# Another order of TensorE's work in the attention loop of a fused attention and mixture-of-experts kernel

## Chip, cores and metric

One core of a Trainium2 chip. The metric is the device time of one execution in microseconds (us). Engines: TensorE (PE, its weight loads PEld), VectorE (DVE), ScalarE (ACT), GpSimd (POOL) and SyncE (SP), which issues most of the transfers.

## What is computed

x is [8, 16, 16, 256]: eight images of 256 positions. First a layer norm over channels and axial attention (every position attends to its row and to its column, with a Gaussian decay), projected and added to x; then a layer norm and a top-1 switch gate over 8 experts with 256 places each.

```python
q, k, v = (xn @ W.T + b for W, b in ((Wq, bq), (Wk, bk), (Wv, bv)))
r_attn = softmax(einsum('bhwd,bhkd->bhwk', q, k) - gw * dist(w))
c_attn = softmax(einsum('bhwd,bgwd->bwhg', q, k) - gw * dist(h))
x = x + ((r_attn @ v) + (c_attn @ v)) @ Wo.T + bo
idx = argmax(softmax(t @ wg))                  # t = layer norm of x, one token a row
loc = cumsum(one_hot(idx), axis=0) - 1         # place of a token at its expert, below 256
out = x + gate * (relu(di @ w1[e]) @ w2[e])    # di: the tokens of expert e
```

## The kernel before

The kernel has a preparation (weights folded together), a loop over the eight images (the attention and the gate), and then the eight experts. The change is in the loop over images; each engine has its program written out by hand, and semaphores tie them together. Image i is two tiles of 128 positions.

TensorE's helpers for an image i (line numbers as in the trace):

- transpose_x(i) (L599): four transposes of the normalised image `xn` into the PSUM bank bank_xT. ScalarE copies them to xT_high (L859), VectorE subtracts to get xT_low (x_low, L1070).
- query(i) (L580, L581, L587 into bank_q): twelve matmuls in three passes for each half (high x high, high x low, low x high). The third pass of the first half waits for xT_low.
- scores(i) (the same lines into bank_s): twelve matmuls of query and transposed x. VectorE's maxima(i) (L1124, L1127) read them, ScalarE takes the exponentials (L883, L884), and VectorE's weights(i) (L1137 to L1140) joins row and column weights into e_col.
- transpose_prob(i) (L639): four transposes of e_col into bank_pT, copied by ScalarE (L870).
- values(i) (into banks_v): twelve matmuls of 274 columns, copied by ScalarE (L890). It waits for v_ready >= i and for count_read >= i - 1.
- attention_out(i, t), "the product" (L650 into banks_o): weights times values, eight matmul instructions in all. VectorE's residual(i, t) (L1154) reads it and makes the row of the new x.
- counts(i) (L661 to L665): five small matmuls that count, from the chosen experts of image i and of those before, how many tokens chose each expert. Their output is ps_count, a piece of the bank of the values, or, with late=True, ps_count_late, a piece of bank_xT. Without late it also waits for v_ready >= i + 2.

VectorE's turn i is: x_low(i + 1), maxima(i), place(i - 2), weights(i), query_low(i + 1), residual(i - 1), choose(i - 1). choose (L1162 to L1167) takes the maximum of the gate's logits (lmax), `ranked`, rmax and `chosen`. place (L1173 to L1181) forms `both`, multiplies the counts out of PSUM (`counted`, which raises count_read), and ends in `slot`.

ScalarE's turn i is: transposed_x(i + 1), normalised_x(i + 2), transposed_prob(i - 1), exponentials(i), query(i + 1), one piece of an expert weight, values(i).

GpSimd works for i = 2 to 7 on: pre_residual(i - 1) (four small operations, L461 to L465, behind ScalarE's copy of the values), x_and_bias(i) (L471, waits for xT_high_ready >= min(i + 2, 8) and for x2_ready >= 2 (i - 1), the residuals of image i - 2), for i = 3 to 6 a piece of expert 1's weights (L487), and scatter_rows(i - 2) (two indirect DMAs, L478, behind `slot`).

The loop of TensorE runs over i = 1 to 6 (B is 8); the last image is done after it. The expert phase behind it begins with the rows that the last images send.

Of the kernel before, what the change touches and what calls it, by code (L numbers as in the profile page):

```python
# [33 lines left out]
B, HH, WW, D = 8, 16, 16, 256  # L34
# [17 lines left out]
EARLY = B - 2  # L52
# [37 lines left out]
def wait(eng, sem, value):  # L90

    if isinstance(value, int) and value <= 0:
        return
    eng.wait_ge(sem, value)
# [18 lines left out]
def build(nc, x, Wq, bq, Wk, bk, Wv, bv, Wo, bo, sigma, wg, w1, w2, tables_in, eye, tokens, slots, out):  # L113
    f32, f32r, bf16, i32, u32 = mybir.dt.float32, mybir.dt.float32r, mybir.dt.bfloat16, mybir.dt.int32, mybir.dt.uint32
    ALU, ACT, AX = mybir.AluOpType, mybir.ActivationFunctionType, mybir.AxisListType

    ctx = ExitStack()
    with ctx:
        def sb(name, shape, dt=f32):
            return ctx.enter_context(nc.sbuf_tensor(name, shape, dt))  # L120
# [4 lines left out]
        def sem(name):  # L125
            return ctx.enter_context(nc.semaphore(name))
# [58 lines left out]
        chosen = sb("chosen", [P, 2, E], bf16)  # L185
        both = sb("both", [P, E], bf16)
        before = [sb(f"before{j}", [P, E], bf16) for j in range(2)]
        counted, loc = sb("counted", [P, 2, E]), sb("loc", [P, 2])
# [22 lines left out]
        def halves(a):  # L211
            return a.rearrange("p (a b) -> p a b", a=2)
# [6 lines left out]
        ps_count = halves(ps_v[:, 0, MW:MW + 2 * E])  # L219
        ps_count_late = halves(bank_xT[:, 0:2 * E])  # L220
# [47 lines left out]
        chosen_ready, count_made, count_read, slot_ready = (sem(n) for n in ("chosen_ready", "count_made", "count_read", "slot_ready"))  # L268
# [37 lines left out]
        def pT_of(i, t):  # L306
            return ps_pT_last[t] if i == B - 1 else ps_pT
# [256 lines left out]
        def _(pe):  # L564
# [6 lines left out]
            def three_passes(out_ap, stationary, moving, last="moving", before_last=None, before_pair=None):  # L571


                n = len(stationary)
                for c in range(n):
                    (a_h, a_l), (b_h, b_l) = stationary[c], moving[c]
                    second = (a_h, b_l) if last == "stationary" else (a_l, b_h)
                    if before_pair and c % 2 == 0:
                        before_pair(c // 2)
                    nc.tensor.matmul(out_ap, a_h, b_h, start=c == 0, stop=False)  # L580
                    nc.tensor.matmul(out_ap, *second, start=False, stop=False)  # L581
                if before_last:
                    before_last()
                for c in range(n):
                    (a_h, a_l), (b_h, b_l) = stationary[c], moving[c]
                    third = (a_l, b_h) if last == "stationary" else (a_h, b_l)
                    step = nc.tensor.matmul(out_ap, *third, start=False, stop=c == n - 1)  # L587
                return step
# [4 lines left out]
            def transpose_x(i):  # L593

                pe.wait_ge(xn_ready, i + 1)
                wait(pe, xT_ready, i)
                for t in range(2):
                    for c in range(DC):
                        step = nc.tensor.transpose(ps_xT[:, c, t * P:(t + 1) * P], xn[:, t, c * P:(c + 1) * P], ident)  # L599
                step.then_inc(xT_made, 1)  # L600

            def query(i):
                j = i % 2
                pe.wait_ge(xT_high_ready, i + 1)
                wait(pe, q_ready, i)
                for d in range(DC):
                    step = three_passes(ps_q[:, d, :], [(a_high[:, c, chunk[d]], a_low[:, c, chunk[d]]) for c in range(DC)],
                                        [(xT_high[j][:, c, :], xT_low[j][:, c, :]) for c in range(DC)],
                                        before_last=(lambda: pe.wait_ge(xT_ready, i + 1)) if d == 0 else None)
                step.then_inc(q_made, 1)  # L610

            def scores(i):

                j = i % 2
                pe.wait_ge(q_high_ready, i + 1)
                wait(pe, top_ready, 4 * i)
                for t in range(2):
                    three_passes(scores_of(i, t), [(qT_high[:, c, chunk[t]], qT_low[:, c, chunk[t]]) for c in range(DC)],
                                 [(xT_high[j][:, c, :], xT_low[j][:, c, :]) for c in range(DC)], last="stationary",
                                 before_last=(lambda: pe.wait_ge(q_ready, i + 1)) if t == 0 else None).then_inc(s_made, 1)  # L620

            def values(i, which=range(2)):

                j = i % 2
                wait(pe, v_ready, i)
                wait(pe, count_read, i - 1)
                for t in which:
                    step = three_passes(ps_v[:, t, 0:MW], [(xT_high[j][:, c, chunk[t]], xT_low[j][:, c, chunk[t]]) for c in range(DC)],
                                        [(m_high[:, c, :], m_low[:, c, :]) for c in range(DC)])
                    if t == 1 or i == B - 1:  # L630
                        step.then_inc(v_made, 1)

            def transpose_prob(i, which=range(2)):

                wait(pe, pT_ready, 2 * i)
                for t in which:
                    pe.wait_ge(u_ready, 2 * i + t + 1)
                    for c in range(2):
                        step = nc.tensor.transpose(pT_of(i, t)[:, c, t * P:(t + 1) * P], e_col[:, t, c * P:(c + 1) * P], ident)  # L639
                    step.then_inc(pT_made, 1)  # L640

            def attention_out(i, t):

                pe.wait_ge(pT_ready, 2 * i + (t + 1 if i == B - 1 else 2))
                pe.wait_ge(v_ready, i + 1 + (i == B - 1))
                wait(pe, x2_ready, 2 * (i - 1) + t + 1)
                if i == 0:
                    pe.wait_ge(b_ready, 1)
                for c in range(2):
                    step = nc.tensor.matmul(ps_o[:, t, 0:VW], pT[:, c, t * P:(t + 1) * P], v_sb[i % 2][:, c, 0:VW], start=c == 0, stop=c == 1)  # L650
                step.then_inc(o_made, 1)

            def counts(i, late=False):

                pe.wait_ge(chosen_ready, i + 1)
                wait(pe, before_ready, i)
                wait(pe, count_read, i)
                if not late:
                    pe.wait_ge(v_ready, i + 2)
                ps, b = ps_count_late if late else ps_count, before[i % 2]  # L660
                nc.tensor.matmul(ps[:, 0, :], upper, chosen[:, 0, :], start=True, stop=False)  # L661
                nc.tensor.matmul(ps[:, 0, :], ones[:, :], b[:, :], start=False, stop=True)
                nc.tensor.matmul(ps[:, 1, :], upper, chosen[:, 1, :], start=True, stop=False)
                nc.tensor.matmul(ps[:, 1, :], ones[:, :], chosen[:, 0, :], start=False, stop=False)
                nc.tensor.matmul(ps[:, 1, :], ones[:, :], b[:, :], start=False, stop=True).then_inc(count_made, 1)  # L665
# [64 lines left out]
            query(1)  # L730
            pe.wait_ge(m_ready, 1)
            values(0)
            for i in range(1, B - 1):
                transpose_x(i + 1)
                scores(i)
                transpose_prob(i - 1)
                query(i + 1)
                if i > 1:
                    counts(i - 2)
                attention_out(i - 1, 0)  # L740
                attention_out(i - 1, 1)
                values(i)


            transpose_prob(B - 2)
            scores(B - 1)
            counts(B - 3)
            attention_out(B - 2, 0)
# [297 lines left out]
        def _(dve):  # L1046
# [122 lines left out]
            def place(i, target):  # L1169

                j = i % 2
                dve.wait_ge(chosen_ready, i + 1)
                route.mark(nc.vector.tensor_tensor(both[:, :], chosen[:, 0, :], chosen[:, 1, :], ALU.add))  # L1173
                dve.wait_ge(count_made, i + 1)
                nc.vector.tensor_tensor(counted[:, :, :], ps_count_late if i >= EARLY else ps_count, chosen[:, :, :], ALU.mult).then_inc(count_read, 1)
                route.done()
                if i < B - 1:
                    nc.vector.tensor_tensor(before[1 - j][:, :], before[j][:, :], both[:, :], ALU.add).then_inc(before_ready, 1)
                dve.wait_ge(count_read, i + 1)
                route.done(nc.vector.tensor_reduce(loc[:, :], counted[:, :, :], axis=AX.X, op=ALU.add))  # L1180
                return nc.vector.scalar_tensor_tensor(target[:, :], loc[:, :], float(E), rmax[:, :], ALU.mult, ALU.subtract)  # L1181
# [168 lines left out]
```

## Time and profile before

| | us |
|---|---|
| median of 3 runs | 191.82 (191.21 to 193.5) |
| the profiled execution | 190.23 |
| its span | 188.4 |
| TensorE busy | 176.1 |
| VectorE busy | 146.8 |
| GpSimd busy | 115.6 |
| ScalarE busy | 112.6 |

The profile is one execution. Its page gives busy times of the engines; the timeline gives start and length of each instruction in us from the span's start, merged where one form repeats (x4 is four instructions), and in brackets the idle time before it with what ended it. A matmul's length overlaps with that of the next one, so its cost in flow is the distance from start to start.

### The profile page before, as it was taken

Reading aid. Unit: us, or ns where it says so; the run is one execution under the profiler, and the core shown is the slowest. Engines: PE = TensorE matmul, PEld = TensorE weight load, DVE = VectorE, ACT = ScalarE, POOL = GpSimd, SP = SyncE. Lnnn points to the kernel's source line nnn. Section 1 sums busy time; section 2 is a strip of 40 time slices with the busy share of each in tenths; the row PEclk is TensorE's granted clock in tenths of the full one; section 3 lists DMA queues with packets and bytes.
Section 4 is the critical chain, followed back from the end, with each engine's and each line's share of the span. In section 5 each row is a group of like instructions: output and inputs, shape, how many; then the busy total and the mean of one; then the engine's idle time right before and its main releaser. Section 6 shows DMA issues by size and latency. Waiting matters only on the chain.

```text
span 188.4 us, 3903 instructions
## 1 busy us (share of the span) xinstructions
PE 176.1 (93%) x1356; PEld 168.9 (90%) x1356; DVE 146.8 (78%) x422; ACT 112.6 (60%) x273; POOL 115.6 (61%) x139
## 2 busy tenths in 40 slices
PE   7699999799999999998999899999999999999880
PEld 7598889699999998778999899999999999999870
DVE  0577999999999989634647899999799994997820
ACT  3258777577878587523839894881957915745000
POOL 4334976276866856567049779748377484368652
PEclk9988999999999999999999999999999999999997
DMA  5799995111311316576698439058193293601010
GB/s 176 225 398 347 283 291 222 57 61 57 115 61 56 114 61 214 188 215 233 187 343 245 177 105 357 28 159 317 60 350 118 41 349 135 230 2 46 3 67 28
DMA packets 23829, 31.67 MB, mean 168 GB/s; under 512 B 2696, under 2 KB 20617, under 8 KB 23808
## 3 DMA queue, kind: packets, MB, share of 16 engines
q1 hardware_dynamic: 21232, 26.32, 43.1%
q0 software_dynamic: 1616, 4.24, 6.4%
q10 hardware_dynamic: 960, 0.85, 1.3%
q8 instruction: 11, 0.18, 0.4%
q14 instruction: 10, 0.08, 0.1%
HBM read 23.02 MB, written 8.55 MB: 168 GB/s over the span
## 4 chain that ended last, share of the span: by engine, by line
PE 76%; DVE 12%; DMA 3%; issue 3%; ACT 2%; SPq 1%; POOLq 1%; DVEq 0%
PE banks_v L580 7%; PE banks_v L581 7%; PE banks_v L587 7%; PE banks_o L650 6%; PE bank_q L587 4%; PE bank_pT L587 4%; PE bank_pT L580 4%; PE bank_pT L581 4%; PE bank_q L580 3%; PE bank_q L581 3%; DMA wg_sb<-in_L_ffn_wg 3%; PE bank_s L587 3%; PE bank_s L580 3%; PE bank_s L581 3%; PE bank_xT L587 2%
## 5 line engine op out<-in xcount | busy, mean ns | idle before, releaser
L904 ACT ACTIVATE w_high<-w_in_sb 128x1024 fp32r<-128x1024 f32 x22 | 22.8, 1056 | 3.3 <-DMA w_in_sb<-in_L_ffn_w 3.3
L539 POOL DMA_INDIRECT out<-y,goal x16 | 16.7, 1043 | 11.8 <-issue 8.0
L521 POOL TENSOR_TENSOR w_low<-vx,w_high 128x1024 fp32r<-128x1024 f32 x8 | 20.1, 2538 | 5.2 <-ACT w_high L904 5.2
L521 POOL TENSOR_TENSOR w_low<-w_in_sb,w_high 128x1024 fp32r<-128x1024 f32 x7 | 16.7, 2403 | 10.2 <-ACT w_high L904 10.1
L478 POOL DMA_INDIRECT slots<-row,slot x14 | 14.1, 1009 | 14.2 <-DVE slot L1181 11.2
L1264 DVE TENSOR_TENSOR w_low<-w_in_sb,w_high 128x1024 fp32r<-128x1024 f32 x12 | 16.1, 1343 | 5.3 <-ACT w_high L904 5.1
L650 PE MATMUL banks_o<-vx,pT 128*128 128x266 f32 x64 | 16.4, 397 | 0.3 <-issue 0.3
L580 PE MATMUL banks_v<-w_high,h_high 128*128 128x256 f32 x64 | 16.0, 287 | 0.0
L1005 ACT ACTIVATE h_high<-bank_xT 128x512 fp32r<-128x512 f32 x8 | 4.7, 593 | 18.7 <-PE bank_xT L587 18.7
L581 PE MATMUL banks_v<-w_high,h_low 128*128 128x256 f32 x64 | 15.7, 283 | 0.0
L580 PE MATMUL bank_pT<-w_high,h_high 128*128 128x256 f32 x56 | 14.0, 287 | 0.0
L581 PE MATMUL bank_pT<-w_high,h_low 128*128 128x256 f32 x56 | 13.7, 283 | 0.0
L650 PEld LDWEIGHTS banks_o<-vx,pT 128*128 128x128 f32 x64 | 11.4, 189 | 2.1 <-issue 0.5
L1279 DVE TENSOR_TENSOR gate_g<-ginv,rstd_g 128x2 f32<-128x2 f32 x8 | 13.0, 1627 | 0.3
L580 PEld LDWEIGHTS banks_v<-w_high,h_high 128*128 128x128 f32 x64 | 12.3, 191 | 0.2 <-DVE h_low L1272 0.2
L1281 DVE CAST goal<-sl 128x2 int32<-128x2 f32 x8 | 12.2, 1522 | 0.3
L581 PEld LDWEIGHTS banks_v<-w_high,h_low 128*128 128x128 f32 x64 | 12.3, 191 | 0.0
L431 POOL TENSOR_TENSOR rstd<-var_eps,minus_half 128x2 f32<-128x2 f32 (+1 forms) x6 | 4.9, 808 | 11.3 <-DVE var_eps L1067 11.3
L848 ACT ACTIVATE xn<-sl,nmr,rstd 128x256 f32<-128x256 f32 x16 | 8.7, 597 | 4.3 <-POOL nmr L433 4.3
L471 POOL TENSOR_TENSOR vx<-sl,obias 128x512 f32<-128x512 f32 x8 | 10.3, 1283 | 1.1 <-DVE obias L1119 0.9
L580 PEld LDWEIGHTS bank_pT<-w_high,h_high 128*128 128x128 f32 x56 | 10.7, 191 | 0.0
L581 PEld LDWEIGHTS bank_pT<-w_high,h_low 128*128 128x128 f32 x56 | 10.7, 191 | 0.0
(243 smaller groups left out, 658.6 us busy)
## 6 DMA issues: line engine op xcount, KB each, us to landing
w_in_sb<-in_L_ffn_w SPq DMA_DIRECT2D x12, 1024.0 KB, 6.9
vx<-in_L_ffn_w SPq DMA_DIRECT2D x4, 1024.0 KB
sl<-slots SPq DMA_DIRECT2D x9, 266.0 KB, 4.5
slots<-empty SPq DMA_DIRECT2D x8, 266.0 KB, 8.1
out<-row SPq DMA_DIRECT2D x7, 256.0 KB, 2.3
sl<-in_x SPq DMA_DIRECT2D x4, 256.0 KB, 5.7
sl<-in_x SPq DMA_DIRECT2D x2, 512.0 KB, 8.8
table_in<-in_tables SPq DMA_DIRECT2D x1, 292.0 KB, 5.4
```

The costliest lines, as they stand in the source:

```text
L471: nc.gpsimd.tensor_tensor(xb[i % 2][:, :, 0:D], x_sb[:, tiles(i), :], obias[:, None, :].to_broadcast([P, 2, D]), ALU.add).then_inc(xb_read ...
L478: nc.gpsimd.indirect_dma_start(slot_rows, bass.IndirectOffsetOnAxis(ap=slot_of(i)[:, t:t + 1].bitcast(u32), axis=0), row_of(i)[:, t, :], N ...
L521: step = nc.gpsimd.tensor_tensor(w2_low[e % 2][:, half, :], w2_raw[e % 2][:, half, :], w2_high[e % 2][:, half, :].bitcast(f32), ALU.subtract)
L539: nc.gpsimd.indirect_dma_start(out_rows, bass.IndirectOffsetOnAxis(ap=goal[j][:, c:c + 1].bitcast(u32), axis=0), y[j][:, c, :], None, boun ...
L580: nc.tensor.matmul(out_ap, a_h, b_h, start=c == 0, stop=False)
L581: nc.tensor.matmul(out_ap, *second, start=False, stop=False)
L587: step = nc.tensor.matmul(out_ap, *third, start=False, stop=c == n - 1)
L650: step = nc.tensor.matmul(ps_o[:, t, 0:VW], pT[:, c, t * P:(t + 1) * P], v_sb[i % 2][:, c, 0:VW], start=c == 0, stop=c == 1)
L904: nc.scalar.activation(high[e % 2][:, half, :], raw[:, half, :], ACT.Copy).then_inc(ready, 1)
L1264: step = nc.vector.tensor_tensor(w1_low[e % 2][:, c, :], w1_in_sb[:, c, :], w1_high[e % 2][:, c, :].bitcast(f32), ALU.subtract)
L1279: gate.done(nc.vector.tensor_tensor(gate_g[:, tiles(e)], ginv[:, tiles(e)], rstd_g[:, tiles(e)], ALU.mult))
L1281: nc.vector.tensor_copy(goal[j][:, :], sl[:, tiles(e), COL_TOK]).then_inc(goal_ready, 1)
```

## The change

TensorE's turn i was: transposes of x(i + 1), scores(i), transposes of the weights of image i - 1, query(i + 1), counts(i - 2), product(i - 1), values(i). It becomes: scores(i), query(i + 1), counts(i - 2), values(i), product(i - 1), transposes of x(i + 2), transposes of the weights of image i. The transposes of x(2) go ahead of the loop. The counts of the turns go to bank_xT (late), so the transposes of x(i + 2) wait until VectorE has read them. values keeps its wait for count_read. The orders of the other engines are as before.

```diff
             values(0)
+            transpose_x(2)
             for i in range(1, B - 1):
-                transpose_x(i + 1)
                 scores(i)
-                transpose_prob(i - 1)
+                if i == 1:
+                    transpose_prob(0)
                 query(i + 1)
                 if i > 1:
-                    counts(i - 2)
+                    counts(i - 2, late=True)
+                values(i)
                 attention_out(i - 1, 0)
                 attention_out(i - 1, 1)
-                values(i)
-
-
-            transpose_prob(B - 2)
+                if i + 2 < B:
+                    wait(pe, count_read, i - 1)
+                    transpose_x(i + 2)
+                transpose_prob(i)
+
+
             scores(B - 1)
             counts(B - 3)
...
-                nc.vector.tensor_tensor(counted[:, :, :], ps_count_late if i >= EARLY else ps_count, chosen[:, :, :], ALU.mult).then_inc(count_read, 1)
+                nc.vector.tensor_tensor(counted[:, :, :], ps_count if i == B - 3 else ps_count_late, chosen[:, :, :], ALU.mult).then_inc(count_read, 1)
```

## Rows read from the trace of the kernel before

**Rows 1.** The page's part 1, TensorE: busy us, share of the span, instructions.

```profile
PE 176.1 (93%) x1356; PEld 168.9 (90%) x1356; DVE 146.8 (78%) x422; ACT 112.6 (60%) x273; POOL 115.6 (61%) x139
```

**Rows 2.** Busy time by stretch, one steady turn: busy us (instructions), clock, DMA.

```profile
54.60:61.90 7.30, 7.30 (x60) 6.97 (x59) 6.75 (x30) 5.67 (x16) 5.20 (x9) 1.00 0.22 77
```

**Rows 3.** Timeline of TensorE, turn 5: start us, us, line, operation, count.

```profile
54.61 0.60 PE L599 MATMUL bank_xT<-ident,xn 128*128 128x128 f32 x4
54.96 0.36 PE L580 MATMUL bank_s<-xT_high,qT_high 128*128 128x256 f32 x1
...
56.48 0.60 PE L639 MATMUL bank_pT<-ident,e_col 128*128 128x128 f32 x4
56.84 0.36 PE L580 MATMUL bank_q<-xT_high,a_high 128*128 128x256 f32 x1
...
58.34 0.18 PE L661 MATMUL banks_v<-chosen,table_in 128*128 128x8 bf16 x1
...
58.48 2.04 PE L650 MATMUL banks_o<-vx,pT 128*128 128x266 f32 x8
60.16 0.48 PE L580 MATMUL banks_v<-m_high,xT_high 128*128 128x274 f32 x1
...
61.88 0.60 PE L599 MATMUL bank_xT<-ident,xn 128*128 128x128 f32 x4
```

**Rows 4.** Timeline of TensorE, turns 1 and 2.

```profile
23.63 0.66 PE L599 MATMUL bank_xT<-ident,xn 128*128 128x128 f32 x4 [0.39 <-ACT xn L848]
...
27.89 1.96 PE L650 MATMUL banks_o<-vx,pT 128*128 128x266 f32 x8
...
35.47 0.50 PE L587 MATMUL bank_q<-xT_low,a_high 128*128 128x256 f32 x2 [1.29 <-DVE xT_low L1070]
...
36.52 0.18 PE L661 MATMUL banks_v<-chosen,table_in 128*128 128x8 bf16 x1
```

**Rows 5.** Timeline of VectorE, turns 1 and 2.

```profile
31.93 0.89 DVE L1154 SCALAR_TENSOR_TENSOR row<-banks_o,einv,vx 128x266 f32<-128x266 f32 x2
...
33.06 1.34 DVE L1164 SCALAR_TENSOR_TENSOR ranked<-row,lmax,table_in 128x8 f32<-128x8 f32 x2
...
34.73 0.68 DVE L1070 TENSOR_TENSOR xT_low<-bank_xT,xT_high 128x512 fp32r<-128x512 f32 x1
...
36.84 0.17 DVE L1175 TENSOR_TENSOR counted<-banks_v,chosen 128x16 f32<-128x16 f32 x1 [0.24 <-PE banks_v L665]
...
37.25 0.16 DVE L1181 SCALAR_TENSOR_TENSOR slot<-loc,rmax 128x2 int32<-128x2 f32 x1
```

**Rows 6.** Timeline of GpSimd, turns 1, 2 and 5.

```profile
32.96 1.28 POOL L471 TENSOR_TENSOR vx<-sl,obias 128x512 f32<-128x512 f32 x1
...
40.99 0.21 POOL L461 TENSOR_TENSOR vx<-vx,std 128x16 f32<-128x16 f32 x1 [0.18 <-issue]
...
41.43 0.22 POOL L465 TENSOR_TENSOR vx<-vx,ow 128x16 f32<-128x16 f32 x1
...
57.39 1.29 POOL L487 TENSOR_TENSOR w_low<-w_in_sb,w_high 128x512 fp32r<-128x512 f32 x1
```

**Rows 7.** Timeline of VectorE, turn 5.

```profile
57.95 0.75 DVE L1173 TENSOR_TENSOR both<-chosen 128x8 bf16<-128x8 bf16 x1
...
62.17 0.17 DVE L1162 TENSOR_REDUCE lmax<-row 128x2 f32<-128x16 f32 x1
62.38 0.36 DVE L1164 SCALAR_TENSOR_TENSOR ranked<-row,lmax,table_in 128x8 f32<-128x8 f32 x2
...
62.98 0.20 DVE L1167 TENSOR_TENSOR chosen<-table_in,rmax 128x16 bf16<-128x16 bf16 x1
```

**Rows 8.** Timeline of ScalarE, turn 1: high part of a transposed x.

```profile
24.33 0.60 ACT L859 ACTIVATE xT_high<-bank_xT 128x512 fp32r<-128x512 f32 x1 [0.23 <-PE bank_xT L599]
```

**Rows 9.** Timeline of VectorE, the last image after the loop.

```profile
70.66 0.42 DVE L1124 CUSTOM_DVE_ANT_0 s_col<-bank_s,mask_col 128x256 f32<-128x256 f32 x1 [0.21 <-PE bank_s L587]
...
72.47 0.42 DVE L1124 CUSTOM_DVE_ANT_0 s_col<-bank_xT,mask_col 128x256 f32<-128x256 f32 x1
```

## Prediction

> **What bounds the kernel now.** Three views, in this order. The page's first part says that TensorE is busy nearly all the time [rows 1]. The busy time by stretch says where there is anything to win: in one steady turn of the attention loop TensorE is busy the whole stretch, at the full granted clock, and VectorE for 6.75 of 7.30 us [rows 2]. So the steady turns are bound by TensorE with VectorE close behind. The timelines then show what each engine does in a turn and who waits for whom.
>
> A turn of TensorE lasts 61.88 - 54.61 = 7.27 us [rows 3]. Its parts, start to start: transposes of x 0.35, scores 1.52, transposes of weights 0.36, query 1.50, counts 0.14, product 1.68, values 1.72. After a stall, eight matmuls of 256 columns took 36.52 - 35.47 = 1.05 us, the first pair 0.10 us longer than in flow (0.50 against 0.40) [rows 4]; so 0.95 for eight, 1.43 for twelve. Scores and query therefore carry 0.08 each of the transposes ahead of them, and a group of four transposes really costs 0.43. Product and values are 3.40 together.
>
> **The change part by part.** No instruction is added or removed except one wait, and no DMA is issued from elsewhere. Turns 2 to 6 are those in which the new order differs with counts in it.
>
> *Order itself.* The same groups in another order cost TensorE the same, when nothing stalls: 1.43 + 1.43 + 0.14 + 3.40 + 2 x 0.43 = 7.26 against 7.27. I take 0, with 0.1 a turn as the bound to either side.
>
> *Counts, then values, with nothing between.* values(i) still waits for count_read >= i - 1, which is VectorE's reading of counts(i - 2) from PSUM (`counted`). Before, the product stood between them and hid this. VectorE starts `counted` 0.32 us after the counts start (36.52 to 36.84) and runs 0.17 [rows 4, 5]; TensorE follows VectorE after 0.06 (xT_low ends at 34.73 + 0.68 = 35.41, TensorE resumes at 35.47) [rows 4, 5]. So values start 0.55 after counts, not 0.14: 0.41 lost, a turn. Bound below: 0.35; above: 0.55 with 0.10 of restart. Let C be the start of counts. Values: 12 matmuls of 274 columns, 1.53 (12 x 0.1275: the 1.72 of the row without the 0.19 that belongs to the product's tail), plus 0.10 restart: the product starts at A = C + 0.55 + 1.63 = C + 2.18.
>
> *The product late, so the residual late.* VectorE's residual(i - 1) reads it, and behind the residual on VectorE stand choose(i - 1), then x_low(i + 2), for which the third pass of query(i + 2) waits. The product ends at A + 1.96 [rows 4]; a reader starts 0.04 after an end (transposes end 23.63 + 0.66 = 24.29, ScalarE starts 24.33) [rows 4, 8]. The second residual starts at A + 2.00; two overlapping ones take 0.89 from the first start, so one some 0.49 [rows 5]; so lmax at A + 2.52, and with the distances 62.17, 62.38, 62.98 `ranked` at A + 2.73 and `chosen` at A + 3.33, done by A + 3.53 [rows 7]. x_low would start at A + 3.58 and let the third pass go 0.74 later (34.73 to 35.47) [rows 4, 5], at A + 4.32. TensorE is there at A + 1.77 (product) + 0.86 (two groups of transposes) - 0.08 + 1.52 + 0.48 = A + 4.55. So without anything else VectorE's chain fits, by 0.23 us only.
>
> *The transposes of x early, so GpSimd's large addition early.* x_and_bias (L471, 1.28 us) waits for the transposed x that ScalarE copies (xT_high) and for the residual. Now the transposes follow the product: done at A + 1.96 + 0.43 = A + 2.39, copied A + 2.43 to A + 3.03 [rows 8], GpSimd may start at A + 3.07. GpSimd is free: slot(i - 2) starts at 37.25 = C + 0.73 now; from C to the first operation behind the two scatters is 40.99 - 36.52 = 4.47, to the end of the small ones 41.65 - 36.52 = 5.13 = A + 2.95; `counted` keeps its 0.32 behind the counts, so this distance holds [rows 4, 5, 6]. So L471 runs about A + 3.10 to A + 4.40, exactly over `chosen` at A + 3.33.
>
> What does that cost? The trace of before shows two VectorE operations that read two SBUF tensors under a large GpSimd operation: `ranked`, 1.34 us for a pair that takes 0.36, until L471 ended at 34.24 [rows 5, 6, 7]; and `both`, 0.75, until L487 ended at 57.39 + 1.29 = 58.68 [rows 6, 7]. `chosen` never lay under one. It reads two SBUF tensors too, so I take it as caught; the other bound is that it runs on in 0.20. Caught: it ends at about A + 4.45, x_low starts at A + 4.50, the query resumes at A + 5.24 and next counts start 1.05 later, A + 6.29 = C + 8.47. The turn is 8.47, 1.20 longer, with a stall of the query of 5.24 - 4.55 = 0.69 and 0.10 of restart beside the 0.41. If GpSimd gets in between the two `ranked` instead, the second ends at A + 4.45 and x_low starts 0.43 later: 1.6 a turn.
>
> The Trainium skill (SBUF — State Buffer, "Who interferes with whom") says that a VectorE instruction with two SBUF inputs and a GpSimd instruction that reads SBUF exclude each other, the later one waiting for the whole of the earlier; the rows on `ranked` and `both` agree with it. By that rule `chosen` is caught, and the sum would be +5.8; if the rule did not reach `chosen`, +2.0.
>
> *Turns 0 and 1.* transpose_x(2) stands where it stood (TensorE waited for xn at 23.63 [rows 4]). In turn 1 values(1) and the product change places, and VectorE does the same work: residual(0) at 31.93 comes after other work on VectorE, `ranked` is caught at 33.06, x_low(3) starts at 34.73, and query(3) waits for it until 35.47 [rows 4, 5]. By then TensorE has done the same groups in either order. Counts(0) start at 36.52 in both: 0.
>
> *Sum to the end of the loop.* From counts(0) at 36.52, four turns of 8.47 bring counts(4); before, four of 7.27: +4.8. After them values, product, transposes of weights and scores(7) lose the 0.40 once more: +5.2.
>
> *After the loop.* Before, maxima of the last image start at 70.66, and the second one's at 72.47, 1.81 later, of which about 0.6 is `both` caught under L471 [rows 9, 7]. New: counts(4) at 36.52 + 4 x 8.47 = 70.40, A = 72.58, choose(5) ends caught at A + 4.45 = 77.0, maxima at 77.1, the second one's 1.2 later, as GpSimd is done by then: 78.3, +5.8. Everything behind hangs on this chain and keeps its length: transposes, product, dispatch and experts move whole.
>
> **Total: +5.8 us.** The profiled execution of before took 190.23 us (span 188.4), so 196.0 for it; the median of the runs is 191.82, so 197.6, 3.0% more.
>
> **Rivals.** *R1, not slower by what can be told: `chosen` is not caught.* Place: choose in turns 2 to 5; it holds if a broadcast operand makes `chosen` immune, or if L471 starts after A + 3.33, 0.26 later than I place it (a scatter or the copy of xT that much slower). Then only the wait for `counted` is left: 5 x 0.41 = 2.0, giving 193.8, 1.1% more. For it: `chosen` was never seen caught; against it: two neighbours of its kind were, and L471 is long. The same result, if the catch happens in one turn only: +2.8. *R2, nothing at all:* `counted` ends before TensorE gets through the counts, or two boundaries between transposes and other matmuls saved give back 0.1 a turn: 191.8 to 191.3. Against it: `counted` waited for the counts itself in turn 2 (0.24 us) [rows 5]; it can't end earlier. *R3, worse: the second `ranked` is caught too*, because GpSimd's small operations (to A + 2.95) hold up the first at A + 2.73: 1.6 to 1.7 a turn, +8 in all: 199.8. Near: 0.03 us decide it.
>
> **How the numbers follow.** The main case (`chosen` caught in most turns) 0.50, R3 0.16, R1 with the partly caught 0.26, R2 0.05, others 0.03. Predicted 197.6, its own range 196 to 199. The range of 8 in 10 takes in R1 from 193.4 and R3 up to 200.4. About 2% is what a measurement of this kernel can tell from no change, 3.84 us: the main case and R3 lie above it, R1 and R2 within: slower 0.67, same 0.31. Faster by 2% would need 3.8 us out of turns in which TensorE is busy throughout: 0.02.
>
> **What the profile after would show.** If right: the turn (counts to counts) 8.4 to 8.6; values after a wait for `counted` of about 0.4, five times; a stall of the query's third pass for xT_low of 0.7 in turns 3 to 6; `chosen` at some 1.1 us, or one `ranked` at 1.2 (R3); `both` back at 0.16. Turn 7.7 and `chosen` at 0.2 is R1. Turn 7.3 is R2. Wrong altogether if the turns lengthen with no wait of TensorE, or if the stretch behind the loop does not keep its length.

## The result, and the profile after

The changed kernel takes 197.19 us in the median of four runs (195.95 to 198.29), the kernel before 191.51 beside it: the ratio is 1.028, interval 1.018 to 1.038. That is 5.7 us; forecast were 5.8. It is slower for certain; that it is slower by more than 2% is likely, but the interval begins at 1.8%. The profiled execution has a span of 194.9 us, 6.5 more than before.

A stretch of the same length as in [rows 2], 7.30 us with one pair of waits in it: busy time of TensorE, its weight loads, VectorE, ScalarE and GpSimd with their instructions, then the granted clock, the DMA share and GB/s:

```profile
47.30:54.60 7.30, 6.56 (x52) 5.93 (x50) 6.17 (x24) 4.59 (x13) 5.18 (x8) 1.00 0.21 75
```

TensorE was busy for 7.30 of 7.30 us; now it is for 6.56, at the same full clock. It stands still, it is not slower. What it waits for stands in its list of waits (us in total, times, longest):

```profile
PE bank_q L587 <- DVE xT_low L1074: 2.9, 5, 1.4
...
PE banks_v L580 <- DVE counted L1179: 1.8, 5, 0.4
...
PE banks_v L661 <- DVE chosen L1171: 0.7, 1, 0.7
```

The two waits of a turn are the first two lines: five times for xT_low (one of them is the 1.4 of turn 1, which was there before with 1.29, [rows 4]) and five times for `counted`. The third is behind the loop, where the sixth counts wait for `chosen`. A whole turn, timeline of TensorE in the changed kernel (counts to counts; start us, length us, and in brackets the idle time before):

```profile
37.17 0.18 PE L661 MATMUL bank_xT<-chosen,table_in 128*128 128x8 bf16 x1
...
37.81 0.37 PE L580 MATMUL banks_v<-m_high,xT_high 128*128 128x274 f32 x1 [0.36 <-DVE counted L1179]
...
39.42 1.96 PE L650 MATMUL banks_o<-vx,pT 128*128 128x266 f32 x8
41.21 0.60 PE L599 MATMUL bank_xT<-ident,xn 128*128 128x128 f32 x4
...
44.51 0.50 PE L587 MATMUL bank_q<-xT_low,a_high 128*128 128x256 f32 x2 [0.38 <-DVE xT_low L1074]
...
45.56 0.18 PE L661 MATMUL bank_xT<-chosen,table_in 128*128 128x8 bf16 x1
```

The turn is 45.56 - 37.17 = 8.39 us (8.39, 8.39, 8.38, 8.38) where it was 7.27 [rows 3]. Values start 0.64 after the counts and are released by `counted`; the third pass of the query is released by xT_low. VectorE in the same turn:

```profile
37.09 0.16 DVE L1177 TENSOR_TENSOR both<-chosen 128x8 bf16<-128x8 bf16 x1
37.49 0.17 DVE L1179 TENSOR_TENSOR counted<-bank_xT,chosen 128x16 f32<-128x16 f32 x1 [0.24 <-PE bank_xT L665]
...
41.41 0.49 DVE L1158 SCALAR_TENSOR_TENSOR row<-banks_o,einv,vx 128x266 f32<-128x266 f32 x1 [0.40 <-PE banks_o L650]
...
42.15 0.36 DVE L1168 SCALAR_TENSOR_TENSOR ranked<-row,lmax,table_in 128x8 f32<-128x8 f32 x2
...
42.75 1.10 DVE L1171 TENSOR_TENSOR chosen<-table_in,rmax 128x16 bf16<-128x16 bf16 x1
43.78 0.68 DVE L1074 TENSOR_TENSOR xT_low<-bank_xT,xT_high 128x512 fp32r<-128x512 f32 x1
```

and GpSimd:

```profile
41.91 0.22 POOL L465 TENSOR_TENSOR vx<-vx,ow 128x16 f32<-128x16 f32 x1
42.52 1.30 POOL L471 TENSOR_TENSOR vx<-sl,obias 128x512 f32<-128x512 f32 x1 [0.39 <-ACT xT_high L863]
43.78 1.28 POOL L487 TENSOR_TENSOR w_low<-w_in_sb,w_high 128x512 fp32r<-128x512 f32 x1
```

`chosen` should take 0.20 us [rows 7]. It started at 42.75, under L471 (42.52 to 43.82), and ended at 43.85: 1.10 us. An operation of VectorE that is drawn out in this way under one of GpSimd is called caught. xT_low starts when GpSimd is done. `both`, which was the caught one before, at 0.75 [rows 7], takes 0.16. Behind the loop it is the pair `ranked` that is caught (VectorE, the lines that answer to [rows 9]):

```profile
75.68 1.36 DVE L1168 SCALAR_TENSOR_TENSOR ranked<-row,lmax,table_in 128x8 f32<-128x8 f32 x2
...
77.44 0.42 DVE L1128 CUSTOM_DVE_ANT_0 s_col<-bank_s,mask_col 128x256 f32<-128x256 f32 x1
...
78.64 0.42 DVE L1128 CUSTOM_DVE_ANT_0 s_col<-bank_xT,mask_col 128x256 f32<-128x256 f32 x1
```

Where the 6.5 us of the span came from, by stretch:

| stretch | before | after | more |
|---|---|---|---|
| start to first counts | 36.52 | 37.17 | 0.65 |
| first to fifth counts (four turns) | 29.09 | 33.54 | 4.45 |
| fifth counts to first expert matmul | 19.77 | 20.83 | 1.06 |
| experts | 103.02 | 103.36 | 0.34 |

The first line is not the change's. In the preparation GpSimd has one operation of 4.6 us, here in the kernel before (first line) and in the changed one (second line):

```profile
18.98 4.60 POOL L449 TENSOR_TENSOR w_low<-w_in_sb,w_high 128x2048 fp32r<-128x2048 f32 x1
19.64 4.59 POOL L449 TENSOR_TENSOR w_low<-w_in_sb,w_high 128x2048 fp32r<-128x2048 f32 x1
```

It started 0.66 us later in the changed kernel, and from its end to the first counts it is 12.94 us in both (36.52 - 23.58 and 37.17 - 24.23). Its start moves from execution to execution (18.48 to 23.32 us in the twelve traces), as TensorE's wait for the landing of the gate's weights does (0.9 to 2.9 us). So the experiments below are compared from the first counts to the end (151.88 before, 157.73 after: +5.85) and by the turn, beside their times.

Nothing ties the last line to the change either. TensorE stands still once near the end of the experts (before the first matmul into banks_o of the last expert) for a time that the profile puts down to nothing ("issue"): 0.51 us before, 0.89 in the changed kernel, 1.50 in run 3, and none is listed in run 8. That is the 0.34 to within 0.04. It stands in the column "first counts to end" below, so the turns tell more than differences of under 1 us in that column.

### The profile page after: what moved, and what is told of

Same layout as the page of the kernel before. It is cut to its first block, busy times and chain, and to the rows that moved or that the text cites. A ratio compares the mean times of both kernels' runs of the same rounds, so it can differ in the third digit from the quotient of the medians.

```text
span 194.9 us, 3898 instructions
## 1 busy us (share of the span) xinstructions
PE 177.8 (91%) x1356; PEld 169.1 (87%) x1356; DVE 149.1 (77%) x422; ACT 112.5 (58%) x273; POOL 115.9 (59%) x139
## 4 chain that ended last, share of the span: by engine, by line
PE 66%; DVE 19%; issue 4%; ACT 4%; DMA 3%; SPq 1%; POOLq 1%; DVEq 0%; ACTq 0%
PE banks_v L580 8%; PE banks_v L581 7%; PE banks_v L587 7%; PE banks_o L650 5%; PE bank_q L587 4%; PE bank_pT L587 3%; PE bank_pT L580 3%; PE bank_pT L581 3%; DMA wg_sb<-in_L_ffn_wg 3%; PE bank_q L580 3%; PE bank_q L581 3%; DVE row L1158 3%; DVE ranked L1168 2%; DVE chosen L1171 2%; DVE xT_low L1074 2%
## 5 line engine op out<-in xcount | busy, mean ns | idle before, releaser
L887 ACT ACTIVATE e_col<-s_col,ntop 128x256 f32<-128x256 f32 x16 | 8.0, 503 | 10.5 <-DVE ntop L1131 10.5
L471 POOL TENSOR_TENSOR vx<-sl,obias 128x512 f32<-128x512 f32 x8 | 10.4, 1297 | 4.2 <-ACT xT_high L863 2.2
L580 PE MATMUL banks_v<-m_high,xT_high 128*128 128x274 f32 x32 | 9.4, 310 | 1.8 <-DVE counted L1179 1.8
```

What stands on the lines that cost most here:

```text
L471: nc.gpsimd.tensor_tensor(xb[i % 2][:, :, 0:D], x_sb[:, tiles(i), :], obias[:, None, :].to_broadcast([P, 2, D]), ALU.add).then_inc(xb_read ...
```

## The experiments

The theory: two things cost the time, and both come from the product standing behind the values. (1) Values wait for VectorE's reading of the counts, now bare. (2) The residual is late, and the transposes of x follow the product at once, so that GpSimd's addition L471 starts just before `chosen` and holds it up, and with it xT_low and the query. Rival A: the place of the transposes costs it. Rival B: VectorE's own chain is too long, whatever catches it.

| kernel | turn | `chosen` | first counts to end | ratio to before (interval) |
|---|---|---|---|---|
| before | 7.27 | 0.20 | 151.88 | |
| changed | 8.39 | 1.10 | 157.73 | 1.028 (1.018 to 1.038) |
| 1 only product and values swapped | 8.37 | 1.09 | 158.98 | 1.032 (1.024 to 1.041) |
| 2 all but that swap | 7.23 | 0.18 | 151.90 | 0.996 (0.990 to 1.002) |
| 3 changed, no wait for the counts | 7.89 | 1.04 | 156.33 | 1.023 (1.015 to 1.031) |
| 4 changed, addition behind `chosen` | 8.08 | 0.18 | 156.21 | 1.021 (1.011 to 1.030) |
| 5 both, 3 and 4 | 7.20 | 0.17 | 152.27 | 0.999 (0.994 to 1.004) |
| 6 changed, addition in halves | 7.83 | 0.54 | 155.36 | 1.020 (1.011 to 1.030) |
| 7 before, addition behind `chosen` | 7.27 | 0.20 | 151.79 | 0.995 (0.991 to 0.998) |
| 8 as 7, and the last addition later | 7.27 | 0.20 | 150.90 | 0.992 (0.988 to 0.997) |
| 9 as 5, and the last addition later | 7.20 | 0.17 | 151.72 | 0.997 (0.993 to 1.001) |

**1. Only product and values swapped** (the transposes stay where they were before; the edit is shown against the kernel before, without the line that tells VectorE where the counts lie)

```diff
+                wait(pe, count_read, i - 2)
                 transpose_x(i + 1)
...
-                    counts(i - 2)
+                    counts(i - 2, late=True)
+                values(i)
                 attention_out(i - 1, 0)
                 attention_out(i - 1, 1)
-                values(i)
```

> The order of before, with only product and values changing places (and the counts in bank_xT, as the swap needs). The theory (late product, values behind the reading of the counts, `chosen` caught under GpSimd's large addition): the transposes of x again follow the product directly, so the turn from counts to counts is 8.4 us as in the changed kernel, `chosen` takes 1.1 us, and the time is 5 to 6 us over before. Rival A (the place of the transposes, two groups side by side at the end of the turn, costs the time): the turn stays at 7.3 to 7.5 us and the time within 1 us of before.

Measured: the whole loss is there, 196.81 against 191.85 us. Turns 8.37 us, ratio 1.032, and `chosen` on VectorE as in the changed kernel:

```profile
43.12 1.09 DVE L1168 TENSOR_TENSOR chosen<-table_in,rmax 128x16 bf16<-128x16 bf16 x1
```

Only the first turn was longer, 9.89 us; see the last section.

**2. All but that swap**

```diff
+                attention_out(i - 1, 0)
+                attention_out(i - 1, 1)
                 values(i)
-                attention_out(i - 1, 0)
-                attention_out(i - 1, 1)
                 if i + 2 < B:
```

> The changed kernel with product and values back in their old order; the transposes stay at the end of the turn. The theory: the product hides the reading of the counts, the residual comes early and `chosen` is over before GpSimd's addition starts; turn 7.27 us, time as before within 0.5 us. Rival A (the transposes' place): turn 8 us or more, time 4 to 6 us over before.

Measured: no loss (191.89 against 191.85). With the product early, `chosen` is over before the addition starts; VectorE, then GpSimd:

```profile
50.48 0.18 DVE L1171 TENSOR_TENSOR chosen<-table_in,rmax 128x16 bf16<-128x16 bf16 x1
```

```profile
50.73 1.30 POOL L471 TENSOR_TENSOR vx<-sl,obias 128x512 f32<-128x512 f32 x1
```

Runs 1 and 2 together rule rival A out: the transposes may stand at either place, what costs is the order of product and values. Run 2 also has the counts in bank_xT, so that is not the cost either.

**3. The wait for the counts taken away.** Counts of the loop lie in bank_xT, so values(1) to values(6) have nothing to wait for; values(7) keeps the wait, since the counts before it are in the values' bank.

```diff
-                wait(pe, count_read, i - 1)
+                if i == B - 1:
+                    wait(pe, count_read, i - 1)
```

> The changed kernel; values of images 1 to 6 no longer wait for VectorE's reading of the counts, which lie in another bank there. The theory: the wait of 0.36 us goes, the product starts 0.5 us earlier. GpSimd's addition is then held by its own small operations until 4.97 us after the counts and `chosen` comes at 5.03, so who is first is open by 0.1 us. Addition first: turn 8.0 us, time 2 us under the changed kernel. `chosen` first: turn 7.2 to 7.3 us, time as before. Rival B (VectorE's own chain sets the turn, whatever it is caught by): turn stays at 8.3 to 8.4 us.

Measured: the turn fell from 8.39 to 7.89, by 0.50, and `chosen` was still caught. VectorE and GpSimd:

```profile
49.18 1.04 DVE L1172 TENSOR_TENSOR chosen<-table_in,rmax 128x16 bf16<-128x16 bf16 x1
```

```profile
48.55 0.22 POOL L465 TENSOR_TENSOR vx<-vx,ow 128x16 f32<-128x16 f32 x1
48.89 1.30 POOL L471 TENSOR_TENSOR vx<-sl,obias 128x512 f32<-128x512 f32 x1
```

The addition now starts behind GpSimd's own small operations, 0.29 us ahead of `chosen`. So the query still waits; the wait of values was worth 0.5 us a turn. From the start of the product on, the turn is as it was: the addition 3.11 us behind it and `chosen` 3.40 (3.10 and 3.33 in the changed kernel).

**4. The addition behind `chosen`**

```diff
                 wait(pool, x2_ready, 2 * (i - 1))
+                wait(pool, chosen_ready, i - 1)
```

> The changed kernel; GpSimd's large addition waits for `chosen` too. The theory: `chosen` takes 0.2 us, the query's wait for xT_low is gone in turns 3 to 6, the wait of values for the counts stays. The turn would be 7.75 us; GpSimd's next operation (L487, 1.28 us) then lies over `both`, which makes it about 8.0. Time 3 to 4 us under the changed kernel, 2 to 2.5 us over before. Rival B (VectorE's chain sets the turn by its length): turn 8.3 to 8.4 us, and a stall of the query as long as now.

Measured: 194.14 us, and `chosen` back at 0.18. VectorE:

```profile
48.77 0.18 DVE L1172 TENSOR_TENSOR chosen<-table_in,rmax 128x16 bf16<-128x16 bf16 x1
...
51.00 0.67 DVE L1178 TENSOR_TENSOR both<-chosen 128x8 bf16<-128x8 bf16 x1
51.60 0.16 DVE L1180 TENSOR_TENSOR counted<-bank_xT,chosen 128x16 f32<-128x16 f32 x1
```

and GpSimd:

```profile
49.12 1.30 POOL L472 TENSOR_TENSOR vx<-sl,obias 128x512 f32<-128x512 f32 x1 [1.20 <-DVE chosen L1172]
50.38 1.27 POOL L488 TENSOR_TENSOR w_low<-w_in_sb,w_high 128x512 fp32r<-128x512 f32 x1
```

The catch moved on: `both` started at 51.00 under the piece of expert 1's weights (L487, L488 in this kernel; 50.38 to 51.65) and took 0.67, and behind it `counted` and the values came later. The first turn, in which `both` was not caught (0.16), took 7.73 us, the others 8.08: the 7.75 and the 8.0 of the expectation. That contradicts rival B, by which the turn would have stayed at 8.3: VectorE does the same work here, in the same order.

**5. Both edits**

> The changed kernel with both edits: values do not wait for the counts, GpSimd's addition waits for `chosen`. The theory: these two are all that the new order costs, so the turn is 7.2 to 7.3 us; the stall of turn 1 shrinks by 0.8 us as `ranked` is no longer caught there, and the time is 0.5 to 1.5 us under before. Rival B or a cost not yet named: turn 7.6 us or more, time over before.

Measured: the turn is 7.20 us, 0.07 shorter than before, so within the loop the two causes are all, and the new order itself is even a little cheaper. The time was missed, though: 191.67, equal to before, not 0.5 to 1.5 us less. The stall of turn 1 did shrink, to 0.4 us (second line below). The loss is behind the loop, where the fifth counts to the first expert matmul took 20.18 us (19.77 before). `both` took 0.92 us there (0.76 before), under the addition of the last image (72.03 to 73.30), and TensorE waited 0.8 us for e_col, further down VectorE's chain (first line):

```profile
PE bank_pT L641 <- DVE e_col L1146: 0.8, 1, 0.8
...
PE bank_q L588 <- DVE xT_low L1076: 0.4, 1, 0.4
```

**6. The addition in two halves**

```diff
-                nc.gpsimd.tensor_tensor(xb[i % 2][:, :, 0:D], x_sb[:, tiles(i), :],
-                                        obias[:, None, :].to_broadcast([P, 2, D]), ALU.add).then_inc(xb_ready, 1)
+                for t in range(2):
+                    step = nc.gpsimd.tensor_tensor(xb[i % 2][:, t, 0:D], x_sb[:, 2 * i + t, :], obias[:, :], ALU.add)
+                step.then_inc(xb_ready, 1)
```

> The changed kernel; GpSimd's addition of 128x512 is two of 128x256, some 0.65 us each. The theory (an operation of VectorE that reads two SBUF tensors waits for the end of the one GpSimd operation that runs): `chosen` waits for the first half only and takes about 0.4 us, the query's stall goes, turn 7.75 us, time 2.5 to 3.5 us under the changed kernel. If GpSimd keeps what it holds from one half to the next: `chosen` 1.1 us and turn 8.4 us as now.

Measured: `chosen` took 0.54 us, half of the 1.10, and the turn 7.83. VectorE and GpSimd:

```profile
50.65 0.54 DVE L1172 TENSOR_TENSOR chosen<-table_in,rmax 128x16 bf16<-128x16 bf16 x1
51.12 0.68 DVE L1075 TENSOR_TENSOR xT_low<-bank_xT,xT_high 128x512 fp32r<-128x512 f32 x1
```

```profile
50.43 1.44 POOL L472 TENSOR_TENSOR vx<-sl,obias 128x256 f32<-128x256 f32 x2 [0.62 <-ACT xT_high L864]
```

The pair of halves ran from 50.43 to 51.87, and one half takes 0.74 us (median of the sixteen):

```profile
L472 POOL TENSOR_TENSOR vx<-sl,obias x16: 732/740/751, 27.0 to 74.2; 128x256 f32<-128x256 f32 x16
```

So the first half ended at 51.17, and `chosen` at 51.19. VectorE waits for the end of the one GpSimd operation that runs, not for the next one, which was ready behind it. The query no longer waits in the steady turns; the wait of values stays, and the turn is near the 7.75 expected. The time, 195.16 us, is 2.0 under the changed kernel, where 2.5 to 3.5 was expected.

**7. Before, with the addition behind `chosen`.** The edit of run 4 in the kernel before. It was run twice; the rows here and in the table are of the second time. The expectations of the first and the second time:

> The kernel before; GpSimd's large addition waits for `chosen`. In steady turns `chosen` is over anyway, so nothing changes there. In turn 1 `ranked` is no longer caught: the query's stall there goes from 1.3 to about 0.5 us. Theory: 0.8 us under before. If the caught `ranked` was not what held TensorE up: no difference.

> The kernel before with the addition behind `chosen`, once more, for the stall of turn 1 in an execution with TensorE at its full clock. Theory: the query's wait for xT_low in turn 1 is 0.3 to 0.5 us instead of 1.3, and the time is 0.5 to 1 us under before. If the stall is shorter and the time is the same, the gain was taken back later.

Measured: in turn 1 `ranked` takes 0.36 instead of 1.34 [rows 5], and TensorE waits 0.29 us instead of 1.29 [rows 4]. VectorE and TensorE:

```profile
34.72 0.36 DVE L1165 SCALAR_TENSOR_TENSOR ranked<-row,lmax,table_in 128x8 f32<-128x8 f32 x2
...
35.32 0.17 DVE L1168 TENSOR_TENSOR chosen<-table_in,rmax 128x16 bf16<-128x16 bf16 x1
```

```profile
36.15 0.51 PE L588 MATMUL bank_q<-xT_low,a_high 128*128 128x256 f32 x2 [0.29 <-DVE xT_low L1071]
```

The ratios were 0.999 (0.994 to 1.003) and 0.995 (0.991 to 0.998). The second interval lies under 1, the first does not; both hold 0.997. The stall is gone for certain, a gain in time of some 0.5 us is likely. The traces show 1.0 us: from the end of GpSimd's L449 to the first counts it is 11.95 to 11.97 us in all six traces with the addition behind `chosen`, and 12.94 or more in the other six.

**8. As 7, with the last addition behind the slots of image 5**

```diff
+                if i == B - 1:
+                    pool.wait_ge(slot_ready, B - 2)
```

> As the one before it, and the last image's addition waits for the slots of image 5, so that it does not lie over `both` on the chain behind the loop. Theory: `both` takes 0.16 us there instead of 0.76, the second maxima of the last image start about 0.5 us earlier, and the time is 1.2 to 1.4 us under before (0.7%), faster than both kernels.

Measured: 190.40 against 191.71 us, ratio 0.992, faster than both kernels, as expected. The interval lies under 1. `both` behind the loop takes 0.16 us instead of 0.76, and the stretch from the fifth counts to the first expert matmul is 19.34 us instead of 19.77. The 0.5 us that the experts took less (102.47 against 103.02) is the gap near their end that run 8 does not have; nothing ties that to the edit.

```profile
72.60 0.16 DVE L1176 TENSOR_TENSOR both<-chosen 128x8 bf16<-128x8 bf16 x1
```

**9. As 5, with the last addition behind the slots**

> The changed kernel without both waits (values for the counts, the addition over `chosen`) and with the last image's addition behind the slots of image 5. The theory: the turn is 7.20 us as in the run without both waits, 0.07 under before; `both` behind the loop takes 0.16 us instead of 0.92 and the transposes of the last weights wait 0.4 us less. From the first counts to the end 150.5 to 151.0 us, against 151.9 of before, 1.2 to 1.6 us under before in all. If the order itself still costs something behind the loop: 151.5 us or more from the first counts to the end.

Measured: turns of 7.20, but 151.72 us from the first counts to the end, where 150.5 to 151.0 was expected; 190.10 against 190.69 us. That is the case in which, by the expectation, the order itself still costs something behind the loop. The stretch behind the fifth counts fell from 20.18 only to 19.64, while it is 19.34 in run 8. VectorE in run 9, then in run 8:

```profile
69.26 0.18 DVE L1175 TENSOR_TENSOR chosen<-table_in,rmax 128x16 bf16<-128x16 bf16 x1
69.42 0.42 DVE L1132 CUSTOM_DVE_ANT_0 s_col<-bank_s,mask_col 128x256 f32<-128x256 f32 x1
```

```profile
71.63 0.20 DVE L1170 TENSOR_TENSOR chosen<-table_in,rmax 128x16 bf16<-128x16 bf16 x1
72.04 0.42 DVE L1127 CUSTOM_DVE_ANT_0 s_col<-bank_s,mask_col 128x256 f32<-128x256 f32 x1 [0.21 <-PE bank_s L590]
```

In the order of before, `chosen` is over early and the maxima of the last image wait for TensorE's scores; they start 5.05 us behind the fifth counts (72.04 - 66.99). In the new order the product and so `chosen` come later, and the maxima follow `chosen` directly, at 5.34 (69.42 - 64.08). That is the 0.3 us: a price of the order itself, as `chosen` is not caught here. It eats up what the four turns gain (4 x 0.07). The rest of the distance to run 8 lies in the experts (103.28 us against 102.47): 0.51 is the gap near their end, for the other 0.3 no cause is shown. No version of the new order was measurably better than run 8.

## Why the prediction was right, point by point

- *Total.* +5.8 forecast, +5.7 in the medians, +5.85 in the profiles from the first counts on. The mechanism came as forecast; that the sum fits to 0.1 us is partly luck. Loop and stretch behind it brought 4.45 + 1.06 = 5.5, and the 0.34 of the experts, which the forecast put at 0 and which nothing ties to the change, filled up the rest.
- *Order itself at 0, 0.1 to either side:* runs 2 and 5 give 7.23 and 7.20 against 7.27.
- *Values 0.55 behind the counts:* 0.64 by the starts, as the first matmul of the values started 0.15 behind the end of `counted` (37.66 to 37.81), where 0.06 was taken. So the product was at counts + 2.25, not + 2.18. The wait was forecast at 0.41 a turn (0.51 with the restart); run 3 gives 0.50.
- *`chosen` at A + 3.33, the addition at A + 3.10* (A the start of the product): 42.75 - 39.42 = 3.33 and 42.52 - 39.42 = 3.10, to the hundredth. The trace of before held all these distances, since VectorE's chain behind the product keeps its length.
- *`chosen` caught:* yes, in turns 2 to 5, though before it had never lain under a large addition. That was the open point of the forecast, and run 6 shows it to be a wait for the end of one GpSimd operation. The rule of the Trainium skill (SBUF — State Buffer, "Who interferes with whom") held for it: 1.10 us under the addition, 0.18 without.
- *Its price:* too high. xT_low started at A + 4.36, not 4.50, and the query's third pass at A + 5.09, not 5.24. The turn was 8.39 instead of 8.47, and four turns brought 4.45 us, not 4.8. The term that was off is the hand-over from `chosen` to xT_low. `chosen` ended at A + 4.43, near the forecast 4.45, but xT_low started 0.07 before that end (43.78 against 43.85), where I had put it 0.05 behind. The query's stall was forecast at 0.69 and is 0.54 by the starts (A + 5.09 against the A + 4.55 at which TensorE was there); the profile lists 0.38, as it counts idle time from the end of the matmul before.
- *Behind the loop +1.0:* 1.06. But it was the pair `ranked` that was caught there (1.36), as in R3, not `chosen`. No copy of xT holds the addition there, only GpSimd's small operations, and I had placed their end too late: in the steady turns they end some 0.4 us nearer to the counts than the 5.13 taken from turn 2 of before. So the addition started at A + 2.63 (75.58 - 72.95), ahead of `ranked`. It ended earlier too, at A + 3.92, not + 4.40, but `ranked` stands further ahead in the chain than `chosen`; the two errors made up for each other (`chosen` was over at A + 4.50, forecast 4.45), so that 1.06 fits is luck. In the loop the copy of xT hid this error: there the small operations ended at A + 2.71 and before, and it was xT_high that kept the addition at A + 3.10, behind `ranked`.
- *Turns 0 and 1 at 0:* the stall of turn 1 was 1.36 against 1.29. The 0.65 us up to the first counts came from the preparation, where GpSimd's L449 started 0.66 later.
- *R1* (not caught; turn 7.7, 193.8 us) is nearest to run 4 (7.73 in its first turn, then 8.08; 194.14 us), not this kernel. *R2* (nothing) is contradicted by both waits.

## What to carry to other kernels

When an order by hand is changed, follow what was hidden between producer and reader: a wait that costs nothing because one product stands before it costs its whole length when the product moves. Then place the engines' timelines over each other: the catch of a 0.2 us operation of VectorE under a 1.3 us one of GpSimd could be foretold to 0.01 us in the loop from distances in the old trace; behind the loop the same forecast named the wrong operation, since another wait held the large one there. An explicit wait that lets the small operation go first takes the catch away, and the large one cut in halves makes it half as long, but look which operation is caught next.

## What the hardware showed that was not expected

In run 1 the first turn took 9.89 us, the others 8.37. The granted clock in it, against a later stretch of the same execution (busy times, then the clock):

```profile
36.60:39.60 3.00, 2.94 (x13) 2.97 (x14) 2.28 (x10) 2.06 (x7) 1.41 (x2) 0.50 0.05 14
41.50:46.00 4.50, 4.17 (x37) 3.85 (x35) 4.08 (x16) 2.72 (x7) 2.53 (x2) 1.00 0.17 58
```

From 36.6 to 39.6 us TensorE had half its clock, 1.2 GHz instead of 2.4, and its matmuls of the values were slower (from the start of the values to the product 2.87 us, where the changed kernel took 1.61). TensorE had stood still for 1.27 us shortly before, but the changed kernel kept its full clock behind a stall of 1.36, as run 3 did. It is one execution, the cause stays open, and 1.5 us (9.89 - 8.37) of the 158.98 of run 1 are that turn's.

And the hand-over from GpSimd to VectorE costs next to nothing in the profile: `chosen` ended 0.03 us after the addition that held it, and in run 6 it ended 0.02 us after the first half, with the second half ready behind it.

An operation of VectorE that reads a single SBUF tensor was caught too. In the preparation `minus_mean` takes 0.17 us where nothing of GpSimd's lies over it, but 1.30 us under L449, which ended at 24.23:

```profile
22.96 1.30 DVE L1070 TENSOR_SCALAR minus_mean<-mean_var 128x4 f32<-128x4 f32 x1
```
